# Attention passes with maxima on 32 rows, six row and five one-hot buffers; operands in PSUM in ranking and gated pass

## The reference

```python
# block 0, three layers: relational sum, and attention over the edges of each node
e = leaky_relu(el[src] + er[dst], 0.2)             # one score per edge and head
m = segment_max(e, dst)
ex = exp(e - m[dst]); alpha = ex / segment_sum(ex, dst)[dst]
h_gat = segment_sum(alpha[:, :, None] * z[src], dst)
# block 1, gated
w = sigmoid(relu(concat(h[src], h[dst]) @ We1 + be1) @ We2 + be2)
aggr = segment_sum(w * h[src], dst)
# block 2: attention as in block 0, with a term of the edge's features in the score
# block 3: two convolutions, attention with keys and values k[src] + edge, v[src] + edge
```

## Time and profile before

| | us |
|---|---|
| median of three runs | 11741.47 |
| the profiled execution's own time | 11709.46 |
| its span | 11707.7 |
| PE, DVE, ACT, POOL busy | 8126.2, 8894.5, 4025.8, 6805.0 |
| ranking, from 199 to | 1335 |
| first attention pass, from 1855 to | 3006 |
| gated pass, from 6283 to | 7520 |
| first convolution pass, from 9152 to | 10339 |

### The profile page before, as it was taken

One profiled execution on the slowest core, in us unless ns is written; L12 is line 12 of the kernel. 1 busy time (PEld: TensorE's weight loads), 2 busy tenths in 40 slices (PEclk: granted clock), 3 DMA queues, 4 the chain that ended last, 5 costly groups with the idle time before them and its releaser, 6 DMA issues. The chain is left out here.

```text
span 11707.7 us, 167974 instructions
## 1 busy us (share of the span) xinstructions
PE 8126.2 (69%) x50988; PEld 6507.4 (56%) x50988; DVE 8894.5 (76%) x15409; ACT 4025.8 (34%) x10657; POOL 6805.0 (58%) x7047
## 2 busy tenths in 40 slices
PE   3555257887778887788856777547774788868885
PEld 3444224665446665466645666435653677767774
DVE  8666647898569896698966777578888788758886
ACT  0111123333333333333323555323332344424442
POOL 2777404777137772277734777327773577727773
PEclk8555578888888888888877888767676898879896
DMA  5333475444663446634444888612223577857775
GB/s 192 104 104 104 146 284 199 107 107 106 200 228 108 107 107 178 262 108 107 107 65 157 269 271 273 146 30 56 55 56 36 201 263 265 254 138 264 264 266 146
DMA packets 718027, 1884.83 MB, mean 161 GB/s; under 512 B 265961, under 2 KB 324022, under 8 KB 677736
## 3 DMA queue, kind: packets, MB, share of 16 engines
q0 software_dynamic: 306624, 795.04, 27.0%
q1 hardware_dynamic: 410536, 1079.17, 25.4%
HBM read 1284.44 MB, written 589.18 MB: 160 GB/s over the span
## 5 line engine op out<-in xcount | busy, mean ns | idle before, releaser
L1172 POOL DMA_INDIRECT h<-table,edges_ring x3552 | 3361.1, 946 | 1131.5 <-issue 1039.2
L1172 POOL DMA_INDIRECT edges_rows<-table,edges_ring x1944 | 1857.4, 955 | 598.2 <-issue 579.7
L1347 PE MATMUL bank<-h,edges_onehot 128*128 128x260 f32 (+1 forms) x5312 | 1575.1, 456 | 168.0 <-DVE h L1504 126.6
L1347 PEld LDWEIGHTS bank<-h,edges_onehot 128*128 128x128 f32 x5312 | 1177.4, 254 | 457.9 <-DVE h L1504 230.3
L2645 POOL DMA_INDIRECT rec<-dst,slots x782 | 881.8, 1128 | 434.2 <-issue 238.1
L1458 DVE TENSOR_TENSOR_SCAN bank<-edges_fresh,edges_top,bank 4x1024 f32<-4x1024 bf16 x440 | 1026.6, 2333 | 3.3 <-PE bank L1322 3.3
L1465 DVE TENSOR_TENSOR_SCAN edges_top<-edges_fresh,bank 4x1024 f32<-4x1024 bf16 x440 | 995.1, 2262 | 1.1 <-issue 0.5
L1322 PE MATMUL bank<-ident,edges_score 128*4 128x128 f32 x3520 | 646.1, 346 | 495.7 <-DVE edges_score L1498 494.0
L1391 ACT ACTIVATE edges_narrow_onehot<-edges_onehot 128x1024 bf16<-128x1024 f32 x444 | 469.1, 1057 | 1089.7 <-DVE edges_onehot L1147 1089.7
L1687 PE MATMUL bank<-edges_w_e,edge_score 128*128 128x128 f32 x3520 | 802.9, 316 | 0.0
L1172 POOL DMA_INDIRECT acc<-table,edges_ring x664 | 679.2, 1023 | 208.8 <-issue 193.9
(11 more groups left out here) (459 smaller groups left out, 19251.6 us busy)
## 6 DMA issues: line engine op xcount, KB each, us to landing
table<-x SPq DMA_DIRECT2D x154, 1040.0 KB, 5.5
edge_score<-edge_feat SPq DMA_DIRECT2D x220, 512.0 KB
edges_onehot<-onehot_d SPq DMA_DIRECT2D x220, 512.0 KB, 3.7
table<-h SPq DMA_DIRECT2D x77, 1040.0 KB, 7.3
table<-turn_typed_rows SPq DMA_DIRECT2D x63, 1040.0 KB, 8.1
h<-table,edges_ring POOLq DMA_INDIRECT x3552
onehot_d<-edges_onehot SPq DMA_DIRECT2D x110, 512.0 KB, 4.9
flip_d<-edges_onehotT SPq DMA_DIRECT2D x110, 512.0 KB, 6.0
```

The lines of the kernel that those rows point to most:

```text
L1172: pool.indirect_dma_start(out=rows[r][:, j, :], out_offset=None, in_=table, in_offset=bass.IndirectOffsetOnAxis(ap=ring[:, s * ST + j:s * ...
L1347: ins = pe.matmul(sum_b[k % 3], onehot[s][:, j, :], rows[s][:, j, A0:W], start=j == k * GT, stop=j == (k + 1) * GT - 1)
```

## The change

Three parts, and what falls out with them.

**Attention passes.** `attention_edges` takes the form of the convolution pass. A step works on five superblocks, b = n + 1 to o = n - 3. The scores are turned to 32 rows of 128 by one transpose. `find_ends` finds each row's maximum before its first and after its last mark, three small matmuls put these in one line, `link` scans the line (32 long, twice), two matmuls turn it back to 32 starts, and `scan_both` scans the rows, 128 long, forward and back. Ring and one-hots: rows 4 to 6 buffers, one-hots 4 to 5 (three of them in the room of `edge_score`, which the pass of block 2 needs itself). The four group sums have a PSUM place each instead of three. SP loads `marks` and `line`, two transfers for each superblock, instead of `fresh`, one.

**Gated pass.** Copies of `place1` and `we2` are put in PSUM at the start, and ACT writes `gate` there. The four group sums then lie in one bank, so that DVE takes them when all four are made, and PE makes the next four when all are taken.

**Ranking.** `place0` and `earlier` are copied to PSUM at the start (`number_b`, `earlier_b`).

Falling out: `fresh_d` with its preparation in the run marks, the convolution branch of `attention_edges` that nothing calls, and helper functions.

In the attention passes and the helpers:

```diff
-    def full(q, s):
-        n, m = s + 2, s + 1
-        step((q + n // RING, n % RING), (q + m // RING, m % RING), (q, s))
...
+    ROWS, HOTS, EARLY = 6, 5, GPS // 2
...
+        place_b = g.bank[1][:, 512 + 2 * P:512 + 3 * P]
+        sum_b = [g.bank[2 + k // 2][:, k % 2 * 512:k % 2 * 512 + W] for k in range(4)]
...
+            for i in range(-1, NSUPER + 3):
+                step(*[u if 0 <= u < NSUPER else None for u in (i + 1, i, i - 1, i - 2, i - 3)])
...
-                    for j in range(ST):
-                        ins = pe.transpose(score_b[0:HEADS, j * P:(j + 1) * P], score[s][:, j, :], g.ident[:, :])
-                    ins.then_inc(score_turned, 1)
+                    pe.transpose(score_b, score[n % 3][:, :, :].rearrange("p h t -> p (h t)"), g.ident[:, :]
+                                 ).then_inc(score_turned, 1)
...
+                def find_ends(m):
...
+                    for k, at in enumerate((2 * P + 1, 0)):
+                        ins = v.tensor_tensor_reduce(masked[:, k, :], score_b, marks[m % 2][:, at:at + P], 1.0, -BIG,
+                                                     ALU.add, ALU.max, ends[:, k:k + 1])
...
+                def link(m):
...
+                    v.tensor_tensor_scan(linked[:, 0:RUNS], line[s][:, 0:RUNS], line_b[:, 0:RUNS], -BIG, ALU.add, ALU.max)
...
+                def scan_both(m):
...
+                    v.tensor_tensor_scan(rising[s][:, :], marks[s][:, P:2 * P], score_b, init_b[:, 0:1], ALU.add, ALU.max
+                                         ).then_inc(rising_made, 1)
...
+                    v.tensor_tensor_scan(top[:, ::-1], marks[s][:, 2 * P:P:-1], rising[s][:, ::-1], init_b[:, 1:2],
                                          ALU.add, ALU.max).then_inc(top_made, 1)
```

In the gated pass:

```diff
-        sum_b = [g.bank[3][:, at:at + D] for at in (0, D, 512, 512 + D)]
+        sum_b = [g.bank[3][:, k * D:(k + 1) * D] for k in range(GPS)]
+        place_b, we2_b = g.bank[3][:, 512:512 + P], g.bank[3][:, 512 + P:512 + P + D]
+        gate_b = g.bank[2][:, 512 + P:512 + P + ST]
...
-                    if k % 2 == 0:
-                        hold(pe, sums_taken, GPS * (o - 1) + k + 2)
+                        hold(pe, sums_taken, GPS * o)
...
-                    v.wait_ge(sums_made, GPS * o + k // 2 * 2 + 2)
+                    v.wait_ge(sums_made, GPS * (o + 1))
...
-                    v.tensor_tensor(rh, rh, gate[:, :].unsqueeze(2).to_broadcast([P, ST, D]), ALU.mult
+                    v.tensor_tensor(rh, rh, gate_b.unsqueeze(2).to_broadcast([P, ST, D]), ALU.mult
```

In ranking (`numbers` is `number_b` there, and `place0` in the count):

```diff
-                v.tensor_tensor(place_hot[s][:, 0:T, :], place0[:, :].unsqueeze(1).to_broadcast([P, T, P]),
+                v.tensor_tensor(place_hot[s][:, 0:T, :], numbers.unsqueeze(1).to_broadcast([P, T, P]),
...
-                                                         dst_f[:, bass.ds(k * CH + t, 1)], earlier[:, :],
+                                                         dst_f[:, bass.ds(k * CH + t, 1)], earlier_b,
```

In the run marks:

```diff
-                    sp.wait_ge(starts_made, 1)
-                    sp.dma_start(fresh_d[0:SLOTS].rearrange("(u s) -> u s", u=NSUPER), starts[:, :]).then_inc(starts_out, 16)
...
-                    sp.wait_ge(starts_out, 48)
+                    sp.wait_ge(starts_out, 16)
```

More of the change, by code:

```diff
@@ L1233, in attention_edges @@
[L1233 to L1244, removed]
+        gathered, seen = g.gathered, p.gathers_before(ROWS)
@@ L1252, in _ @@
             def _(sp):
[L1253 to L1262, removed]
+                for u in range(NSUPER):
@@ L1367, in step @@
                         spread_dst(n, bins)
-                    if m:
+                    if o is not None:
+                        for k in range(GPS - 2, GPS):
+                            sum_group(o, k)
+                    if m is not None:
                         turn_top(m)
-                    if n and conv is not None:
-                        spread_half(n, 1, bins)
-                    if n:
+                    if n is not None:
                         turn_scores(n)
-                superblocks(pe, step)
+                turns_of(pe, step)
@@ L1562, in _, with step @@
-                onehot_ahead((0, 0))
-                superblocks(v, step)
-def back(qs, by):
-    return (qs[0] + (qs[1] - by) // RING, (qs[1] - by) % RING)
+                    v.tensor_tensor(part, part, sum_b[k % 4], ALU.add).then_inc(sums_taken, 1)
+                def step(b, n, m, w, o):
+                    if w is not None:
+                        subtract_top(w)
+                    if m is not None:
+                        find_ends(m)
+                    if o is not None:
+                        bins = load_bins(v, g, o)
+                        for k in range(EARLY):
+                            add_sums(o, k, bins)
+                    if m is not None:
+                        link(m)
+                    if w is not None:
+                        weigh_rows(w)
+                    if b is not None:
+                        onehot_ahead(b)
+                    if o is not None:
+                        for k in range(EARLY, GPS - 2):
+                            add_sums(o, k, bins)
+                    if m is not None:
+                        scan_both(m)
+                    if n is not None:
+                        make_score(n)
+                    if o is not None:
+                        for k in range(GPS - 2, GPS):
+                            add_sums(o, k, bins)
@@ L1570, in stages @@
+                turns_of(v, step)
 def stages(engine, step, depth):
```

475 lines of the change are left out of this document (183 added, 292 removed).

## The result

The changed kernel takes 11546.34 us (median of three, 11544.76 to 11555.49) against 11741.47 before: a ratio of 0.9841 (95% interval 0.9827 to 0.9855), 195 us less. Its profiled execution took 11544.76 us, 164.7 less than the profiled one of before (11709.46), which was 32 us under the median of its own runs.

The account below looks back on a forecast made before the run. POOL's rate of issuing indirect transfers was taken to bound the attention passes and ranking, with DVE's two-SBUF-operand reads lengthening transfers. Terms -128 - 60 + 6 - 4 = -186 us, against the median 11741.47, gave 11555 us, range 11524 to 11615.

Parts of the forecast that it names:

- POOL's rate is the floor, and DVE's operands stretch it: Edge passes and ranking: POOL's issuing bounds them; transfers started while DVE reads two SBUF operands wait until DVE is done.
- 4 (an operand's place is nothing to POOL): Ranking and gated pass: long scatters come from something else that coincides; only + 6 - 4 remain, 11743 us; chance 0.05.
- 3 (`same` holds the scatters all the same): Ranking: `same` still holds scatters by its other SBUF operands; 42 us stay, about 11597 us; chance 0.06.
- Ranking -128: Ranking: freeing one large SBUF operand each of `place_hot`, `bin_hot` and `same` saves 128 us, ends 115 and 142.
- 3.6 was worked out: Ranking: after the change DVE still waits 3.6 us in each chunk.
- Gated pass -60: Gated pass: three DVE instructions losing one SBUF operand each shorten gathers, saving 60 us, ends 20 and 69.
- Rival 2: Gated pass: bound by its transfers throughout, so only 20 of 60 us come, 11595 us; chance 0.15.
- Attention passes +6: Four attention passes: gather rate unchanged, ends of passes 1 to 2 us longer each; +6 us, ends -6 and +20.
- Run marks -4: Run marks: the wait at `firsts` no longer holds the write of `fresh_d`; -4 us, ends 0 and -7.3.
- More row buffers let POOL run further ahead, but it did not wait for buffers before.: Attention passes: extra row buffers take nothing off the path; "PE bank" waits were only 8.0 us in 664 gathers.
- rival 5: Attention passes: PE-DVE chain makes POOL wait for buffers; gains lost from 10.5 us a superblock, about 11950 at 11.0; chance 0.06.
- DVE's wait at the gathers grown by 2 to 3 us for a superblock.: Attention passes: sign of being right, with DVE's gather wait up 2 to 3 us a superblock and passes staying 1150 us.

Follow-up runs that it names:

- e1: Kernel before with the ranking part of the change alone: 11602.12 us, ratio 0.9891 to the kernel before.
- e2: Kernel before with the gated-pass part of the change alone: 11663.91 us, ratio 0.9944 to the kernel before.
- e4: Kernel before with only ranking's one-hot number table in PSUM, `earlier` staying in SBUF: 11641.13 us, ratio 0.9923 to the kernel before.
- e5: Changed kernel with the attention passes' one-hots reading their table from SBUF again: 11782.55 us, ratio 1.0062 to the kernel before.
- e6: Changed kernel with four row buffers instead of six in the attention passes: 11841.85 us, ratio 1.0106 to the kernel before.
- e3: Kernel before with the attention passes and run marks changed alone: 11741.35 us, ratio 1.001 to the kernel before.
- e8: Kernel before with the ranking and gated parts and unused slots spread over 128 source rows, old attention passes: 11311.03 us, ratio 0.9655 to the kernel before.
- e9: Changed kernel with unused slots spread over 128 source rows, repeated on one chip with the old attention form: 11329.28 us, ratio 0.9669 to the kernel before.
- e7: Changed kernel with unused slots filled with 128 different source rows instead of row 0: 11318.03 us, ratio 0.9662 to the kernel before.

## Why the prediction was right, point by point

The predicted 11555 us stands beside a measured 11546, inside the range.

- *POOL's rate is the floor, and DVE's operands stretch it.* Shown, by e1 and e2 (a term each), by e4 (one operand of ranking's two) and by e5, which brings the loss back in another pass. The trace of before bears it out for other instructions too: none of the 155 gathers that start inside a reduce over one SBUF buffer as long as the one-hot (L1857, 1.22 us) with 0.3 us or more of it left is lengthened, while all 69 scatters that start so inside `place_hot` are, by 1.29 us in the mean. Of the rivals, 4 (an operand's place is nothing to POOL) fell with e1, and 3 (`same` holds the scatters all the same) with e1 against e4: freeing `earlier_b` as well takes another 39 us. The Trainium skill, page "SBUF — State Buffer", section "Who interferes with whom", infers that tensor_tensor spares descriptor generation (`same` and the product with `we2` are other instructions, so that even by it not all of the terms would be nothing). `place_hot`, `bin_hot` and the one-hot are tensor_tensor, and in e4 and e5 moving one of their inputs between SBUF and PSUM moves the transfers between 0.96 and up to 2.28 us. The measurement decides.
- *Ranking -128.* -131.6 in the profile from first to last scatter, -126 in e1. Now DVE waits 241.3 / 72 = 3.4 us for a chunk at the landings, where 3.6 was worked out.
- *Gated pass -60.* -60.8 between first gathers, -65 in e2. Rival 2 (bound by its transfers) is refuted for the body of the pass: the DMA share rose from 0.84 to 0.88 and POOL waited for nothing there. It holds at the end, as the prediction had it: POOL stands 21.3 us before the last superblock (of the 25.3 of "PE bank" above), where the padded rows land. In e5 and e6, which have the same gated pass, that wait is 1.6 us at most, and to the first gather of the next pass it is 1448.6 and 1448.3 us, not longer: the landings set the end whether POOL waits or not.
- *Attention passes +6.* Mis-sized: +25.6 in the profile, a little over its end of +20. Its parts were also wrong. The end from the first use on, which the prediction has growing by 1 to 2 us, became 0.2 to 1.0 us shorter. Instead the stream of gathers, which it left as it was, is 2.5 to 4.1 us longer in each pass, and the first use of the last ones comes 3 to 4 us later behind them.
  - The stream: POOL has three idle times of 1.45 us in each pass (four in the second) that the profile puts down to "issue", where the others are 0.30. That is 3.5 us a pass, 14 of the 25.6. The convolution passes of before have them too (9398.19, 9803.27), its attention passes do not, so they came with the form; why they come was not tried and stays open. A further 0.8 us of the first pass (947 for 946 ns in the mean) is the effect of the long scatters in small: 48 gathers start inside the second scan of `scan_both` (L1397, 0.48 us), which reads `marks` and `rising` from SBUF. Against this, the old form's wait of 2.25 us for PE near the end (2957.66) is gone.
  - The later first use is not settled. In e3 it is 21.7 to 22.6 us behind the last gather, for 20.5 to 21.6 in e1 and e4 with the old form; with the padding spread (e8, e9) it is 1.6 to 2.5 us in both forms. So it hangs on the padded rows, and what delays it beyond that stays open.
  - With the marks and all else of e3, 13 us remain, and 18 in e9 against e8.
- *Run marks -4.* The wait from `first_d` to `firsts` is 5.95 us (1397.25 to 1403.20) for 7.28: -1.3, and -0.7 for a DVE instruction that went, together -2.
- *"More row buffers let POOL run further ahead, but it did not wait for buffers before."* True of the form before, and the wrong question: e6 shows that the new form needs them. With four, rival 5 came true by a wait of POOL for buffers (a superblock of gathers every 11.2 us in block 0, 1230 / 110, against the 10.5 worked out), and the whole change was slower than the kernel before.
- *"DVE's wait at the gathers grown by 2 to 3 us for a superblock."* Wrong as a sign: it grew by 302 / 440 = 0.7. Of the 2.8 us of work that DVE lost in each superblock, (761.4 - 63.8) / 440 = 1.6 went into waits at the sums, between the added hand-overs with PE and ACT (L1429 above), so the slack under the floor is far smaller than DVE's busy time says.

The miss of the sum against its own profile (-186 for -165) is thus the attention term, 20 us. The median of the runs moved by 195, more than the profiles, since the profiled execution of before lay 32 us under the median; e1 to e3, each against many runs, give -178. That the forecast lies 9 us from the measured median is therefore in part luck: the ranking and gated terms were right by their mechanism and to within 5 us, the attention term was 20 us too good, and the three runs of before happened to lie further from the changed kernel than its profile does.

## What to carry to other kernels

Where indirect transfers that POOL issues are the bound, look at the longest transfers in the timeline, not at the mean, and at which DVE instruction ends a fixed time before they do; an operand of that instruction moved to PSUM can be worth more than removing the instruction. An engine's busy time off the path is no gain: 1249 us of DVE work went here, all of it from the attention passes, which lost 13 us by e3 and 18 by e9 against e8; and a deeper pipeline has to be paid in buffers. Padding is work too: spread its addresses.

## What the runs showed of the hardware that was not expected

Gathers that all read one row land slowly: in the changed kernel the lag of the first use behind the last issue of its superblock is 2 to 4 us up to the last six superblocks of the first pass and then 6.6, 9.6, 13.7, 17.6, 21.8 and 24.4 us; it is 1.8 us when the same number of gathers reads 128 rows (e7), at less than half the DMA share (0.29 for 0.69). Why one row is slow, no run shows. An indirect transfer that starts inside a long DVE instruction with two SBUF operands, or up to 0.17 us ahead of it (e5), ends 0.80 to 0.88 us after that instruction, nearly always 0.81 to 0.84, whatever was left of it: up to 1.4 us are lost.
